# Two long attentions: the context's two fp16 parts side by side with a column of ones, and a denominator that comes out of TensorE

## The reference, cut to what matters

```python
scores = jnp.einsum('bhmk,bhnk->bhmn', Q, K)
scores = jnp.where(mask == 0, jnp.float32(-1e+20), scores)       # first attention only
attn = jax.nn.softmax(scores / np.sqrt(D_K).astype(np.float32), axis=-1)
ctx = jnp.einsum('bhmn,bhnv->bhmv', attn, V)
```

## Time and profile before

| what | value |
|---|---|
| median of three executions | 431.19 us |
| the profiled execution's own time | 431.47 us |
| its span, first to last instruction | 429.1 us |
| outside the span | 2.4 us |
| mean granted TensorE clock | 0.98 |
| TensorE busy | 397.4 us, 93% of the span |
| VectorE busy | 319.2 us, 74% |
| ScalarE busy | 284.7 us, 66% |
| GpSimd busy | 202.5 us, 47% |
| first attention, scores of step 0 to last context product | 25.3 to 179.7 us |
| second attention, the same | 224.6 to 371.7 us |

### The profile page before, as it was taken

One profiled execution on the slowest core, in us unless ns is written; L12 is line 12 of the kernel. 1 busy time (PEld: TensorE's weight loads), 2 busy tenths in 40 slices (PEclk: granted clock), 3 DMA queues, 4 the chain that ended last, 5 costly groups with the idle time before them and its releaser, 6 DMA issues.

```text
span 429.1 us, 12061 instructions
## 1 busy us (share of the span) xinstructions
PE 397.4 (93%) x4811; PEld 315.2 (73%) x4811; DVE 319.2 (74%) x865; ACT 284.7 (66%) x557; POOL 202.5 (47%) x125
## 2 busy tenths in 40 slices
PE   6998999999999999999988989999999999899975
PEld 3966677777776778888974667667677778788964
DVE  2498888888887887645749989999888887543544
ACT  3247888788787886643336879888988896533240
POOL 1086897898875551001000657879656660030000
PEclk9599999999999999999999999999999999999989
DMA  8769797989999997960002999999999999600000
GB/s 318 291 191 154 149 174 128 181 136 213 229 180 214 224 180 142 418 258 0 5 2 40 179 172 178 194 189 183 173 214 192 191 196 192 257 2 2 5 0 5
DMA packets 186423, 68.13 MB, mean 159 GB/s; under 512 B 181360, under 2 KB 181888, under 8 KB 185472
## 3 DMA queue, kind: packets, MB, share of 16 engines
q1 hardware_dynamic: 186080, 66.32, 76.1%
q10 hardware_dynamic: 288, 1.05, 0.7%
HBM read 21.90 MB, written 0.03 MB: 51 GB/s over the span
## 4 chain that ended last, share of the span: by engine, by line
PE 36%; DVE 29%; ACT 9%; issue 8%; DMA 8%; POOL 5%; SPq 2%; DVEq 0%; POOLq 0%; ACTq 0%
DVE probs L586 13%; PE ps L498 9%; DMA probsT<-halves 7%; PE ps L466 7%; PE ps L721 4%; ACT probs L530 4%; POOL halves L562 4%; DVE probsT L615 3%; ACT halves L537 3%; SPq L414 2%; DVE U L604 2%; PE ps L1118 2%; PE ps L478 2%; PE ps L1021 2%; DVE den L599 2%
## 5 line engine op out<-in xcount | busy, mean ns | idle before, releaser
L562 POOL TENSOR_TENSOR halves<-probs,halves 128x896 f16<-128x896 f32 x67 | 126.5, 1892 | 81.7 <-ACT halves L537 80.9
L466 PE MATMUL ps<-ctxT_parts,GT_parts 128*128 128x512 f16 (+1 forms) x672 | 145.4, 353 | 10.8 <-DVE negmax L586 9.7
L498 PE MATMUL ps<-ctxN,probsT 128*128 128x128 f16 x2352 | 149.3, 219 | 5.4 <-DMA probsT<-halves 2.9
L498 PEld LDWEIGHTS ps<-ctxN,probsT 128*128 128x128 f16 x2352 | 139.3, 98 | 19.8 <-issue 4.9
L530 ACT ACTIVATE probs<-probs,shifted 128x896 f32<-128x896 f32 x112 | 115.5, 1031 | 12.6 <-DVE shifted L591 12.4
L466 PEld LDWEIGHTS ps<-ctxT_parts,GT_parts 128*128 128x128 f16 x672 | 60.2, 98 | 63.0 <-DVE negmax L586 14.5
L537 ACT CAST halves<-probs 128x896 f16<-128x896 f32 x92 | 84.9, 922 | 0.1
L586 DVE CUSTOM_DVE_ANT_0 probs<-ps,zero,negmax 128x896 f32<-128x896 f32 x56 | 67.4, 1204 | 1.3 <-PE ps L466 1.3
L586 DVE CUSTOM_DVE_ANT_0 probs<-ps,maskb,negmax 128x896 f32<-128x896 f32 x56 | 67.4, 1204 | 1.2 <-POOL halves L562 0.7
L604 DVE SCALAR_TENSOR_TENSOR U<-U,alpha,ps 128x128 f32<-128x128 f32 x112 | 38.3, 342 | 32.3 <-PE ps L498 32.2
L527 ACT ACTIVATE alpha<-negmax 128x1 f32<-128x1 f32 x96 | 28.2, 294 | 41.9 <-DVE negmax L586 41.1
(11 more groups left out here) (346 smaller groups left out, 360.2 us busy)
## 6 DMA issues: line engine op xcount, KB each, us to landing
moe<-in_ctxT SPq DMA_DIRECT2D x7, 448.0 KB, 7.8
moe<-in_mask SPq DMA_DIRECT2D x6, 448.0 KB, 10.8
moe<-in_gateT SPq DMA_DIRECT2D x2, 1024.0 KB, 9.1
moe<-in_upT SPq DMA_DIRECT2D x2, 1024.0 KB, 10.7
moe<-in_downT SPq DMA_DIRECT2D x2, 1024.0 KB, 12.6
moe<-in_fir_long SPq DMA_DIRECT2D x1, 2048.0 KB, 10.9
probsT<-halves SPq DMA_TRANSPOSE x92, 4.6
wv<-in_wv SPq DMA_DIRECT2D x2, 512.0 KB, 4.9
```

The costliest lines, as they stand in the source:

```text
L466: ins = pe.matmul(ps[:, 2 * b + h, 0:width], GT_parts[:, g_part, r * P:(r + 1) * P], ctxT_parts[:, keys:keys + width], start=(g_part == 0 ...
L498: ins = pe.matmul(ps[:, bank, 0:D], probsT_parts[:, b, p_part, k * P:(k + 1) * P], ctxN_parts[:, at:at + D], start=(p_part == 0 and c_part ...
L562: eng.tensor_tensor(halves_of(L, n)[:, 1, :], probs[:, n % BUFS, :], halves_of(L, n)[:, 0, :], ALU.subtract).then_inc(lower_of(L, n)[0], 1)
```

## The change

The two parts of a context tile are laid side by side, with columns of ones: each tile of `ctxN` has a pitch of 272 fp16 elements, 16 of ones, 128 of the upper part and 128 of the lower. The window of 260 columns that starts two elements ahead of the upper part holds two ones, the upper part, the lower part and two ones of the next tile. The context product of a step becomes 7 products of 260 columns (upper probabilities by both parts) and 7 of 130 (lower probabilities by ones and upper part), so 14 and not 21. Column 1 of the result is the sum of the probabilities, that is, the denominator.

So `den`, `chunksum` and the accumulating form of the exponential go. `U` becomes two blocks of 8 tiles by 130 columns; one instruction updates both blocks, of 260 columns, and for the first chunk it is a copy out of PSUM. The reciprocal reads column 1 of block 0 and waits for the `U` of its step. At the end ScalarE doesn't scale `U`: it scales the identity by the reciprocal (`den_diag`, in the memory of `GT_parts`), and TensorE multiplies each block of the row tile by this diagonal, two fp32 products that add up in PSUM, where it transposed one tile. `turn_ctx` issues two DMA transposes of 7 tiles per chunk, because the parts now have separate places. `OT` lies in the second block of `U`. GpSimd clears 1024 columns of `U` for the warm-up, writes the ones, and no longer clears anything between the attentions.

```diff
+CTX_PAD, CTX_PITCH, UW = 16, 16 + 2 * D, D + 2
...
-        ctxN = sb("ctxN", [P, KT * D])
+        ctxN = sb("ctxN", [P, (KT * CTX_PITCH + CTX_PAD) // 2])
...
-        U = sb("U", [P, RT, D])
-        GT = U
+        U = sb("U", [P, 2 * RT * UW])
+        U_blocks = U[:].rearrange("p (b r e) -> p b r e", b=2, r=RT)
+        GT = U[:, 0:RT * D].rearrange("p (r c) -> p r c", r=RT)
+        den_diag = GT_parts[:].rearrange("p h c -> p (h c)").bitcast(F32).rearrange("p (r c) -> p r c", r=RT)
...
-                part = slice(2 * c * CK, 2 * (c + 1) * CK)
                 sp.wait_ge(sem("ctxT_ready"), c + 1)
-                sp.dma_start_transpose(ctxN_parts[:, part].rearrange("p (t d) -> p t d", d=P),
-                                       ctxT_parts[:, part]).then_inc(sem(f"ctxN{c % 2}"), 16)
+                for part in range(2):
+                    sp.dma_start_transpose(
+                        ctxN_tiles[:, c * TC:(c + 1) * TC, CTX_PAD + part * D:CTX_PAD + (part + 1) * D],
+                        ctxT_parts[:, (2 * c + part) * CK:(2 * c + part + 1) * CK]).then_inc(sem(f"ctxN{c % 2}"), 16)
...
-                for p_part, c_part in ((0, 0), (0, 1), (1, 0)):
+                for p_part, width in ((0, 2 * UW), (1, UW)):
                     for k in range(TC):
-                        at = 2 * c * CK + c_part * CK + k * D
-                        ins = pe.matmul(ps[:, bank, 0:D], probsT_parts[:, b, p_part, k * P:(k + 1) * P],
-                                        ctxN_parts[:, at:at + D], start=(p_part == 0 and c_part == 0 and k == 0),
+                        at = (c * TC + k) * CTX_PITCH + CTX_PAD - 2
+                        ins = pe.matmul(ps[:, bank, 0:width], probsT_parts[:, b, p_part, k * P:(k + 1) * P],
+                                        ctxN_parts[:, at:at + width], start=(p_part == 0 and k == 0),
...
-                               scale=-1.0, accum_out=chunksum[:, n:n + 1]).then_inc(sem("exp_done"), 1)
+                               scale=-1.0).then_inc(sem("exp_done"), 1)
...
-                dve.tensor_scalar(den[:, r:r + 1], den[:, r:r + 1], alpha[:, n:n + 1], chunksum[:, n:n + 1],
-                                  ALU.mult, ALU.add).then_inc(sem("den_added"), 1)
-                dve.wait_ge(sem("pv_done"), base + n + 1)
-                if n >= RT:
-                    dve.wait_ge(sem("u_added"), base + n - RT + 1)
-                dve.scalar_tensor_tensor(U[:, r, :], U[:, r, :], alpha[:, n:n + 1],
-                                         ps[:, PV_BANKS[n % len(PV_BANKS)], 0:D], ALU.mult, ALU.add).then_inc(
+                dve.wait_ge(sem("pv_done"), base + n + 1)
+                if n < RT:
+                    dve.tensor_copy(total, given).then_inc(sem("u_added"), 1)
+                    return
+                dve.wait_ge(sem("exp_done"), base + n + 1)
+                dve.wait_ge(sem("u_added"), base + n - RT + 1)
+                dve.scalar_tensor_tensor(total, total, alpha[:, n:n + 1], given, ALU.mult, ALU.add).then_inc(
                     sem("u_added"), 1)
...
-                dve.wait_ge(sem("den_added"), base + (CH - 1) * RT + r + 1)
-                dve.reciprocal(rden[:, r:r + 1], den[:, r:r + 1]).then_inc(sem("den_inverted"), 1)
+                dve.wait_ge(sem("u_added"), base + (CH - 1) * RT + r + 1)
+                dve.reciprocal(rden[:, r:r + 1], U_blocks[:, 0, r, 1:2]).then_inc(sem("den_inverted"), 1)
...
-                ins = pe.transpose(ps[:, bank, col:col + P], U[:, r, :], ident)
+                pe.matmul(ps[:, bank, col:col + P], U_blocks[:, 0, r, 2:UW], den_diag[:, r, :], start=True, stop=False)
+                ins = pe.matmul(ps[:, bank, col:col + P], U_blocks[:, 1, r, 0:D], den_diag[:, r, :], start=False,
+                                stop=True)
...
-                act.wait_ge(sem("u_added"), L * STEPS + (CH - 1) * RT + r + 1)
-                act.activation(U[:, r, :], U[:, r, :], ACT.Copy, scale=rden[:, r:r + 1]).then_inc(sem("u_scaled"), 1)
+                act.activation(den_diag[:, r, :], ident, ACT.Copy, scale=rden[:, r:r + 1]).then_inc(sem("u_scaled"), 1)
...
-            pool.memset(alpha[:, 0:RT], 0.0)
-            pool.memset(den[:], 0.0).then_inc(sem("cleared"), 1)
-            pool.memset(U[:], 0.0).then_inc(sem("cleared"), 1)
+            pool.memset(U[:, 0:RT * D], 0.0).then_inc(sem("cleared"), 1)
+            pool.memset(ctxN_tiles[:, :, 0:CTX_PAD], 1.0)
+            pool.memset(ctxN_parts[:, KT * CTX_PITCH:], 1.0).then_inc(sem("cleared"), 1)
...
-                if i == 2:
-                    pool.wait_ge(sem("u_turned"), 3)
-                    pool.wait_ge(sem("a_shifted"), 1)
-                    pool.memset(den[:], 0.0).then_inc(sem("cleared"), 1)
-                    pool.memset(U[:], 0.0).then_inc(sem("cleared"), 1)
```

More of the change, by code:

```diff
@@ L157, in build @@
         ctxN_parts = ctxN[:].bitcast(F16)
+        ctxN_tiles = ctxN_parts[:, 0:KT * CTX_PITCH].rearrange("p (t e) -> p t e", e=CTX_PITCH)
         zero = sb("zero", [P, 1], BF16)
@@ L219, in build @@
         alpha = sb("alpha", [P, CH * RT])
-        chunksum = sb("chunksum", [P, CH * RT])
-        den = sb("den", [P, RT])
         rden = sb("rden", [P, RT])
-        U = sb("U", [P, RT, D])
-        GT = U
+        U = sb("U", [P, 2 * RT * UW])
+        U_blocks = U[:].rearrange("p (b r e) -> p b r e", b=2, r=RT)
+        GT = U[:, 0:RT * D].rearrange("p (r c) -> p r c", r=RT)
+        den_diag = GT_parts[:].rearrange("p h c -> p (h c)").bitcast(F32).rearrange("p (r c) -> p r c", r=RT)
         UT = sb("UT", [P, RT, P])
@@ L231, in mask_raw @@
             return UT[:].rearrange("p r c -> p (r c)")[:, 0:CK].bitcast(I32)
-        OT = sb("OT", [P, PAIRS, 2, S])
+        OT = U[:, RT * UW:RT * UW + PAIRS * 2 * S].rearrange("p (j a s) -> p j a s", j=PAIRS, a=2)
         QT = OT[:, 0:4, :, :].rearrange("p j a s -> p (j a) s")
@@ L486, in pv @@
                 if L == 0 and n % RT == 0:
-                    pe.wait_ge(sem(f"ctxN{c % 2}"), 16 * (c // 2 + 1))
+                    pe.wait_ge(sem(f"ctxN{c % 2}"), 32 * (c // 2 + 1))
                 if n >= len(PV_BANKS):
@@ L594, in add @@
             def add(n):
[L595 to L605 removed]
+                total = U_blocks[:, :, n % RT, :]
+                given = ps[:, PV_BANKS[n % len(PV_BANKS)], 0:2 * UW].rearrange("p (b e) -> p b e", b=2)
+                dve.wait_ge(sem("pv_done"), base + n + 1)
+                if n < RT:
+                    dve.tensor_copy(total, given).then_inc(sem("u_added"), 1)
+                    return
+                dve.wait_ge(sem("exp_done"), base + n + 1)
+                dve.wait_ge(sem("u_added"), base + n - RT + 1)
+                dve.scalar_tensor_tensor(total, total, alpha[:, n:n + 1], given, ALU.mult, ALU.add).then_inc(
                     sem("u_added"), 1)
             def invert(r):
[L609 to L610 removed]
+                dve.wait_ge(sem("u_added"), base + (CH - 1) * RT + r + 1)
+                dve.reciprocal(rden[:, r:r + 1], U_blocks[:, 0, r, 1:2]).then_inc(sem("den_inverted"), 1)
             def turned_lower(n):
@@ L951, in _ @@
         def _(pe):
-            pe.wait_ge(sem("cleared"), 2)
+            pe.wait_ge(sem("cleared"), 1)
             for _ in range(12):
-                pe.matmul(ps[:, 6, :], U[:, 0, :].bitcast(F16)[:, 0:P],
-                          U[:].rearrange("p r d -> p (r d)").bitcast(F16)[:, 0:4 * P], start=True, stop=True)
+                pe.matmul(ps[:, 6, :], U[:].bitcast(F16)[:, 0:P], U[:].bitcast(F16)[:, 0:4 * P], start=True, stop=True)
             loaded(pe, "cst", "in0")
@@ L1621, in temperature @@
                 seq(dve.reciprocal(rtemp[:], tmpp[:, 3:4]))
-            dve.wait_ge(sem("cleared"), 5)
             dve.wait_ge(sem("zeroed"), 1)
```

## The result

| | before | after |
|---|---|---|
| median | 430.08 us (20 executions, 427.18 to 433.72) | 434.21 us (20 executions, 432.05 to 438.11) |
| ratio after / before, 95% interval | | 1.0104 [1.0082, 1.0126] |
| profiled execution, its own time | 431.47 us | 437.4 us |
| its span | 429.1 us | 435.3 us |

The change makes the kernel slower by 1.04%, which is 430.08 x 0.0104 = 4.5 us. The forecast was 436.5 us with a range of 433.5 to 439.5; from the median shown with the kernel before, 431.19, to it are 5.3 us.

What follows compares the result with a forecast made beforehand. TensorE, busy 93% of the span, was taken as the bound, with some 9.4 us slack. 431.47 - 0.7 (loop) + 0.2 (SP's queue) + 5.8 (ends) = 436.8 profiled, so 436.5 us median; range 433.5 to 439.5.

Steps and rivals of the forecast that it cites:

- The mechanism and the sign: Whole kernel: two fp32 products per row tile at the ends cost most; slower 0.66, same 0.28, faster 0.06.
- rival A: Loop gives more back: all of the -1.5 realised, first chunk's copies cheaper, some -2.5, so 434.2 us; chance 0.2.
- The context product, 0: TensorE in the loop: 14 matmuls of 2730 columns take 1.175 us against 1.17 for 21, so no change.
- Rival C: Context product: if weight loads set the pace, 14 matmuls take 0.78 us, -12.9, so about 424; chance 0.02.
- rival E: TensorE: 260-column matmuls cost as much as 384, +12, 449; or fp32 products cost four transposes, +6.5, 443; chance 0.02.
- `U`: VectorE in the loop: 132 more elements add 0.14 us; `den` and `U` together go from 0.44 to 0.40 us.
- take half: Loop: wide `U` -1.3 and +1.4, accumulator read -1.6, together -1.5 us; halved to -0.7 because TensorE's pace is close.
- The slack, 9.4 us: Both attentions: TensorE idles some 9.4 us; relieving only VectorE and ScalarE can't bring much more.
- Rival B: Loop: wide `U` costs hardly more than narrow, 49 places give -8.8 us, ScalarE -1.6, so 426.6; chance 0.04.
- SP's queue, +0.2 within 0 to +3.2: DMA transposes of context: two of 7 tiles for one of 14, bounds 0 and +3.2 us, taken +0.2.
- rival D: Split transposes cost a full issue more, met once by the chain: +3.2 for the +0.2, so 439.5; chance 0.1.
- The ends, +5.8: Attention ends: row tile 0.47 us for 0.11, +2.87 first, +2.65 second, +0.3 for reciprocals waiting for `U`.

Runs made afterwards that it cites:

- Experiment 1: Kernel before, with only the two fp32 products per row tile at the attention ends in place of one transpose: 436.14 us, ratio 1.0127.
- experiment 2: Kernel after, with the ends as before (block 0 scaled and transposed once, block 1 left out of the result): 430.86 us, ratio 1.0004 to before.
- experiment 3: Kernel after, with VectorE summing the two blocks of `U` at the ends and TensorE transposing once: 430.95 us, ratio 0.9997 to before.
- experiment 7: Experiment 2 with `U` updating only block 0, 130 columns, the 260-column products kept: 424.5 us, ratio 0.9848 to before.
- experiment 10: Experiment 7 once more, narrow `U` with the wide products: 426.94 us, ratio 0.9892 to before.
- experiment 6: Kernel after, with the accumulating exponential and `den` on VectorE put back, result unused: 440.25 us, ratio 1.0211 to before.
- experiment 8: Experiment 4 with more lower parts on VectorE in both attentions: 425.49 us, ratio 0.9873 to before.
- experiment 11: Experiment 8 with VectorE taking the lower part of every odd step in the second attention: 426.79 us, ratio 0.9906 to before.
- experiment 4: Kernel after with only the column of ones: 21 products, `U` of 130 columns, ends as before: 427.61 us, ratio 0.9914 to before.
- Experiment 5: Kernel before, with only the context DMA transposes split, two of 7 tiles for one of 14: 429.73 us, ratio 0.9965.

## Why the prediction was right, point by point

**The mechanism and the sign: right, and shown.** The loss is that each row tile goes through two fp32 products, each twice as dear as the transpose that they replace. Experiment 1 makes it alone, experiments 2 and 3 take it alone away, and the ratios close within their intervals: 1.0127 for the ends, 1.0004 for the rest, 1.0104 for the change.

**The forecast or rival A: the time can't tell.** The median of after, 434.21 us, is just what rival A named (434.2), and not the 436.5 of the forecast. But A was worked out from a median of 431.19 for the kernel before, which over 20 executions is 430.08. By the traces the loop gave back 1.1 us, between the forecast's 0.7 and A's 2.5. (A's own sum, 431.19 - 2.5 + 0.2 + 5.8, makes 434.7; its 434.2 is a slip.) From 430.08 the forecast's sum would make 435.4 and A's 433.6, and 434.21 lies between the two.

**The context product, 0: right.** 1.18 us for the 1.175 worked out. From the first start to the last start of a product there are 1.117 us with 21, 1.127 with 14 wide ones and 1.128 with 21 and the ones. Rival C (weight loads set the pace, 0.78 us) falls with it, and so does the first half of E (260 columns as dear as 384). The Trainium skill's 81 ns per matmul of 128 columns ("TensorE: Matmul & The Clock Gate", "Back-to-back issue gap") isn't borne out by the kernels with 21 products: these stand at 1.17/21 = 56 ns.

**`U`, right as an instruction.** 482 ns where 342 + 140 was said, 0.39 us of VectorE for 0.40. By the forecast a round in the chain with a `U` behind a wait and two in place of `den` and `U` changes by 0.14 - 2 x 0.04 = +0.06. The rounds don't show this as clearly. From one start of waited-for scores to the next, the five of before (46.65 to 99.04 us) take 10.39, 10.39, 10.83, 10.39 and 10.39 us, and the five of after (46.36 to 98.66 us) 10.26, 10.39, 10.74, 10.46 and 10.45: the last two are 0.06 to 0.07 longer, but all five together are 0.09 shorter.

**What the loop makes of it: the net right, its two terms too small.** The forecast had -1.3 + 1.4 - 1.6 = -1.5 and took half, -0.7; the traces have -1.1, with 0.9 of spread. (The same loop has 295.18 us in experiments 2 and 3, and before's has 296.44 in experiment 1; the means are 1.0 apart.) But neither side was a matter of 1.4 us. Priced by the 33 places of the forecast, the wide `U` was 33 x 0.14 + 1.4 = 6.0 us and half of it 3.0; experiments 2, 7 and 10 give 5.4 and 5.0 by the loops, 6.7 and 4.8 by the ratios. `den` and the accumulator were 33 x 0.18 + 1.6 = 7.5 and half of it 3.8; experiment 6 gives 5.0 and 4.6. So "take half, because TensorE's pace lies close behind" was the step that failed, by some 2 us or more for the wide `U` and by about 1 for `den`. It doesn't show in the net because the two sides are nearly of one size and of opposite sign, which was luck. The count of places was sound: the chain of before has `den` 31 times where the forecast had 33. Of the 112 x 0.14 = 15.7 us that the wide `U` adds to VectorE about a third reaches the end of the loops.

**The slack, 9.4 us: no run went past it.** The best loops (experiments 7, 8, 11) are 5.4 to 6.0 us below before, and TensorE's idle time in the stretch from 46 to 110 us is then down from 2.6 to 1.1 (experiment 7) and 0.7 us (experiments 4 and 8). Rival B (faster, if `U` costs hardly more) was told right in its condition and too large in its price: with a `U` of 347 ns the loops gain 4.2 to 5.8 us, not 8.8 + 1.6. None of the runs gained more than the slack; whether what is left of it can be had wasn't tried.

**SP's queue, +0.2 within 0 to +3.2: the low end.** Experiment 5 has 0.9965 [0.9921, 1.0008], so +0.4 us at most by this interval, and +0.55 by the loops, within their scatter; rival D falls.

**The ends, +5.8: right, two small terms off against each other.** The fp32 product takes 0.23 us (1.83 / 8) for the 0.235 of the forecast, so a row tile costs 0.46 for 0.47. That makes +1.39 and +1.05 of the first attention's +1.44 and +1.07. The end there is +2.79 for +2.87, in the second +2.74 for +2.65. The +0.3 for the reciprocals doesn't show beside these in after; with the ends short +0.56 stand there with the wide `U` (experiment 2) and +0.29 with the narrow one (experiments 4 and 7). The second half of rival E (four times a transpose) falls: 0.23 for 0.11, two times. The Trainium skill's "4× faster for FP32" for the transpose mode ("TensorE: Matmul & The Clock Gate", "Terms") doesn't fit this row, if it is meant against an fp32 matmul.

**The total.** Predicted +5.3 us over the profiled execution, measured +4.5 [3.5, 5.4] by the ratio. What the traces show, 5.5 - 1.1 = +4.4, agrees with that. The difference of 0.9 is the SP term (0.2), the loop (0.4) and the ends (0.3).

## What to carry to other kernels

Ask of a fused form what it adds at the instruction that the slower chain passes through in each step: here the column of ones was the gain (0.9914 and, once more, 0.9927 by itself), and the wider `U` that came with the fused product gave all of that back (5.0 to 5.4 us by the loops). Work at the end of a phase, where one engine works alone, counts in full: 16 row tiles with some 0.35 us more each made +5.5 us, whereas 15.7 us more on VectorE in the loop made about 5. And a net that is right can hide two terms that are both too small; here it took an experiment on each of them alone to show it.

## What the runs showed of the hardware

**TensorE's clock in the start and near the end differs between executions of one kernel.** The windows of after over its first 24 us (granted clock: third from the end) and of experiment 8, whose program is the same up to there:

```profile
0.00:10.00 10.00, 6.35 (x22) 3.00 (x22) 2.04 (x6) 3.34 (x5) 2.67 (x13) 0.98 0.81 313
10.00:24.00 14.00, 13.91 (x82) 13.38 (x82) 7.73 (x21) 3.29 (x9) 1.51 (x2) 0.53 0.62 243
```

```profile
0.00:10.00 10.00, 6.52 (x22) 2.77 (x22) 1.82 (x6) 3.23 (x4) 2.67 (x13) 1.00 0.82 308
10.00:24.00 14.00, 12.79 (x104) 11.05 (x102) 11.22 (x26) 4.00 (x9) 5.10 (x3) 0.88 0.83 282
```

The lower level (1.2 GHz) held for about (1 - 0.53) / 0.5 x 14 = 13 us in the one and 3.4 in the other, behind idle stretches of 1.92 and 1.75 us between the warm-up products and the first turn at 8.6 and 8.8 us; the clock fell just ahead of 10 us in the one and behind it in the other. The first scores then start at 25.45 or at 21.8 us, 3.7 us apart, and this difference goes through to the end. Near the end, after and before:

```profile
417.00:424.00 7.00, 6.67 (x36) 6.18 (x36) 2.87 (x13) 1.70 (x3) 0.72 (x1) 0.60 0.01 2
```

```profile
411.00:418.60 7.60, 7.03 (x51) 6.58 (x52) 3.81 (x18) 3.06 (x4) 0.72 (x1) 0.78 0.00 0
```

Here the chain has a wait of 4.21 us in after and of 2.72 in before, behind a small piece on GpSimd (L1351 in the one, L1355 in the other). It is TensorE that is waited for: both kernels give it 14 fp32 products there whose only use is to keep it busy, 28 instructions in the trace, and the next real product stands behind them. The timeline of TensorE in after and in before:

```profile
416.39 6.31 PE L722 MATMUL ps<-cst 128*128 128x128 f32 x28
422.63 0.33 PE L1223 MATMUL ps<-cst,moe 64*64 64x64 f32 x4
```

```profile
411.58 5.02 PE L721 MATMUL ps<-cst 128*128 128x128 f32 x28
```

The same 28 instructions take 6.31 us where more of them fall into the lower level, and 5.02 us where fewer do. All thirteen traces fall into two lots there: the rest behind the output product takes 54.7 to 54.9 us or 56.1 to 56.4. Both lots appear with and without the change (experiment 4 has 54.8, its repeat 56.1), so this is no effect of it. It means that single executions of this kernel can lie 5 us apart (3.7 at the start, 1.5 near the end) with nothing changed, and that a difference of 1% must be read from stretches between fixed cuts, or from many executions.

**Matmuls of 128, 130 and 260 columns keep one price per column.** At the higher clock level, 2688 columns in 21 matmuls 1.17 us, 2730 in 14 1.18; an odd start (28 bytes into a tile of 544) made no difference that shows.
